# Scan layer and expert FFN on one core: new places for the first group's projections, for u x D, for the last sigmoid and for one FFN layer

## The chip, the cores and the metric

One core of one Trainium2 chip. The metric is the device time of one execution of the program in microseconds (us), the median of repeated runs.

## The reference, cut to what matters

32 sequences of 128 tokens, 128 features, all in fp32. Each goes through a rotation and a layer norm, a two-directional selective scan ("Mamba") with 256 channels and 16 states, a gated linear unit, a per-sequence low-rank expert layer, and an FFN of width 512:

```python
xc = conv(xi) + conv_b;  u = silu(xc)                     # forward, and reversed in time
dt, Bm, Cm = split(u @ x_proj_w.T)
delta = softplus(dt @ dt_proj_w.T + dt_proj_b)
h = exp(delta * A[n]) * h + (delta * u) * Bm[n]           # for each of 16 states n
y = sum over n of Cm[n] * h  +  u * D                     # u x D, the "skip"
y = y * silu(z);  o = gelu(both directions @ out_proj, dim_reduce)
g = o @ glu_w.T + glu_b;  x1 = g[:128] * sigmoid(g[128:]) + residuals
c = experts(x1)                                           # hid = relu(..), wo
f = silu(gate(c)) * up(c);  f = gelu(h1(f));  f = gelu(h2(f));  out = x1 + w3(f)
```

## The kernel before, in words

**Groups and units.** The sequences are taken in nine groups: group 0 and group 8 have 2 sequences (width 256), groups 1 to 7 have 4 (width 512). A group has 32 **units**: 16 states forward, then 16 in reverse; a unit handles both channel halves at once, so its tiles are 128 x 512 in the outer groups and 128 x 1024 in the inner ones. For a unit, POOL forms the drive du x B (L555), ScalarE the decay exp(delta x A) into one of two PSUM banks (L702), VectorE runs the scan along time (L905) and weighs it with C (L910); for 7 of the 32 units POOL does the weighing (L560) after a scan at L903. TensorE adds the units up by transposing each into `bank_y` (`sum_states`, L1190).

**Around the units.** After the 16th unit of a direction ScalarE copies `bank_y` out (`copy_y`, L708), TensorE turns it back and adds u x D with a matmul against a diagonal (`turn_y`, L1199 for the product, L1201 for the turn), and VectorE multiplies by silu(z) (`gate_y`, L921). All other TensorE work goes through two PSUM banks, `bank_m`: a **fill** is one product into the bank that is next in a fixed order, a **take** is ScalarE's (or VectorE's) read of it, and a fill waits until the fill two before it has been taken. Names of fills: norm, uf0, uf1, ur0, ur1 (convolution, forward and reverse, two halves), z0, z1, dbc, dt (steps and B, C), out, glu1, glu0, res, hid, wo, gate, up, h1, h2 (each of the last in four chunks), w3, tok. A group's front part (norm to dt) runs while the group before is scanned, its back part (out to tok) while the next is scanned. The last group's back part has nothing behind it: that is the **last chain**.

**The order of the work** is written out by a half-unit clock. Tables `FILL`, `TAKE_LAG`, `ACT_AT`, `VEC`, `GPS`, `LOADS`, `SETUP` give each step a time in units, and `FIRST_GROUP`, `NEXT_TO_LAST` and `LAST_GROUP` shift it for groups 0, 7 and 8 (`slot`, L131). Each engine walks the same clock (`timeline`, L354) and issues what has come due, so the tables fix only the order on each engine; semaphores do the rest. `SETUP` places the fills that merge the eight experts' low-rank factors (wi0 to wi7, wo0 to wo7) into full matrices, which VectorE takes (`merge`, L958), and `fuse`, one product of two weights.

**ScalarE's tables.** exp and ln are in one set of activation tables, silu in a second, gelu in a third; `use_table` (L584) loads a set where the next operation needs another (L586). From group 1 on, silu of both u's is one pass after the takes (`silu_front`, L651); in group 0 it is applied in each take (L644). In the last group gelu and silu are applied in the takes, elsewhere in one pass over four chunks (`gelu`, L754; `DIRECT`, L105). The sigmoid is exp at the take (L719), then ln and exp (L721 to L728).

**SP's queue** issues every DMA in the same clock: B and C are stored to memory by `store_bc` (L411) once dbc is taken, and read back as broadcast rows, and x, expert matrices and outputs go the same way.

**Group 0's way to the first scan.** rotation constants; VectorE's `conv_weights` (L878) and `skip_weights` (L873), then `rotate` (L880); POOL's power; ScalarE's `normalise`; norm; z1, z0, uf1, ur0, uf0, ur1 (the six fills in this order); dbc0, dt01, dt00; softplus (L685); POOL's `step_sizes` (delta, L535) and `inputs` (du, L544); then units.

## Time and profile before

| | |
|---|---|
| Median of 3 runs | 1063.78 us (1063.17 to 1065.88) |
| The profiled execution | 1062.9 us, span of its profile 1060.6 us |
| First scan of group 0 / 1 / 8 | 34.65 / 110.74 / 924.74 us |
| Last weighing ends, then the last chain | 1001.6 us, 59.0 us to the end |
| Busy share of the span | TensorE 89%, VectorE 86%, POOL 78%, ScalarE 73% |
| Granted TensorE clock, mean | 0.96 of full speed |

A row of the timeline reads: start, length, engine, line, operation, output<-input, shapes, number of instructions, and in brackets how long the engine had been idle and what released it. A matmul of fp32 stands as two instructions.

### The profile page before, as it was taken

To read this page: it belongs to the slowest core of one execution; us is meant where nothing else is said; L and a number is where in the kernel's file an instruction comes from. 1 tells how busy PE (TensorE), PEld (TensorE's weight loads), DVE (VectorE), ACT (ScalarE), POOL (GpSimd) and SP (SyncE) were. 2 spreads that over 40 slices of the span, in tenths; PEclk is the share of its full clock that TensorE was granted. 3 is DMA by queue.
4 is the path that set the end of the run, shared out by engine and by line. 5 is a ranking of instruction groups with operands and counts; after the bars stand their busy time and mean duration, and the time that the engine had idled before them with its cause. 6 is when DMAs were issued, how large, how long until landed. Compare 5 with 4: busy or idle time off the path is not lost.

```text
span 1060.6 us, 13662 instructions
## 1 busy us (share of the span) xinstructions
PE 943.8 (89%) x4312; PEld 599.0 (56%) x4312; DVE 908.4 (86%) x718; ACT 778.1 (73%) x1233; POOL 829.5 (78%) x430
## 2 busy tenths in 40 slices
PE   5698678778999899999999999999999988998987
PEld 3455455656655467445755566545755575556455
DVE  1788999999999989999999999998999999968600
ACT  4757667778698768877688868877788758777532
POOL 0767998989988897989878997979878998866300
PEclk9697699898999999999999999999999999999999
DMA  3766675463646555654556554745555465536000
GB/s 95 253 204 208 187 216 180 137 218 116 195 142 194 171 165 147 208 167 144 160 163 183 168 167 123 237 147 168 153 164 187 151 178 146 165 121 169 0 11 6
DMA packets 97670, 167.43 MB, mean 158 GB/s; under 512 B 9920, under 2 KB 33408, under 8 KB 97344
## 3 DMA queue, kind: packets, MB, share of 16 engines
q1 hardware_dynamic: 97600, 166.57, 50.8%
q8 instruction: 35, 0.57, 0.2%
q14 instruction: 35, 0.29, 0.1%
HBM read 159.19 MB, written 7.34 MB: 157 GB/s over the span
## 4 chain that ended last, share of the span: by engine, by line
PE 46%; DVE 19%; ACT 17%; issue 15%; POOL 3%; DMA 0%; DVEq 0%; SPq 0%; POOLq 0%; ACTq 0%
DVE bank_d L905 12%; PE bank_m L1102 9%; PE bank_m L1026 9%; PE bank_y L1190 8%; ACT L586 5%; ACT bank_d L702 5%; PE bank_m L1109 5%; PE bank_m L1116 2%; DVE state L903 2%; PE bank_m L1075 2%; PE bank_m L1084 2%; DVE state L910 2%; POOL state L555 2%; PE bank_m L1044 1%; PE bank_m L1059 1%
## 5 line engine op out<-in xcount | busy, mean ns | idle before, releaser
L555 POOL TENSOR_TENSOR state<-du,b_rows 128x1024 f32<-128x1024 f32 (+1 forms) x288 | 603.9, 2121 | 92.6 <-PE bank_y L1190 91.7
L905 DVE TENSOR_TENSOR_SCAN bank_d<-bank_d,state 128x1024 f32<-128x1024 f32 (+1 forms) x225 | 461.2, 2050 | 44.0 <-ACT bank_d L702 38.6
L702 ACT ACTIVATE bank_d<-delta,a_neg 128x512 f32<-128x512 f32 (+1 forms) x576 | 345.0, 634 | 104.5 <-DVE state L910 94.2
L1190 PEld LDWEIGHTS bank_y<-ident,state 128*128 128x128 f32 x2048 | 240.4, 145 | 81.7 <-issue 55.5
L1190 PE MATMUL bank_y<-ident,state 128*128 128x128 f32 x2048 | 263.3, 281 | 17.8 <-POOL state L560 11.7
L910 DVE TENSOR_TENSOR state<-bank_d,c_rows 128x1024 f32<-128x1024 f32 (+1 forms) x225 | 248.8, 1106 | 7.8
L560 POOL TENSOR_TENSOR state<-state,c_rows 128x1024 f32<-128x1024 f32 (+1 forms) x63 | 134.2, 2131 | 16.4 <-DVE state L903 16.4
L903 DVE TENSOR_TENSOR_SCAN state<-bank_d,state 128x1024 f32<-128x1024 f32 (+1 forms) x63 | 128.7, 2042 | 1.2 <-ACT bank_d L702 1.2
L1109 PE MATMUL bank_m<-hidA,h_s 128*128 128x512 f32 (+1 forms) x256 | 111.8, 584 | 15.6 <-ACT relu_dt L683 9.7
L1026 PE MATMUL bank_m<-xnT,w_conv 128*128 128x508 f32 (+7 forms) x288 | 115.3, 550 | 4.8 <-DVE x1T L930 3.1
L1102 PE MATMUL bank_m<-hidB,h_s 128*128 128x512 f32 (+1 forms) x256 | 110.3, 584 | 1.7 <-DVE hidB L944 0.8
L586 ACT ACT_TABLE_LOAD x69 | 88.5, 1283 | 1.9 <-PEq L1266 0.7
L1109 PEld LDWEIGHTS bank_m<-hidA,h_s 128*128 128x128 f32 x256 | 48.3, 197 | 69.3 <-issue 50.7
L1026 PEld LDWEIGHTS bank_m<-xnT,w_conv 128*128 128x128 f32 x288 | 54.1, 195 | 51.0 <-issue 43.1
L1102 PEld LDWEIGHTS bank_m<-hidB,h_s 128*128 128x128 f32 x256 | 48.5, 194 | 56.0 <-issue 52.3
L535 POOL TENSOR_TENSOR delta<-relu_dt,log_dt 128x1024 f32<-128x1024 f32 (+1 forms) x18 | 38.2, 2122 | 24.5 <-ACT log_dt L693 24.5
L1044 PE MATMUL bank_m<-dbc,w_dt_s 64*128 64x512 f32 (+1 forms) x72 | 37.5, 612 | 15.0 <-ACT dbc L677 12.6
L751 ACT ACTIVATE hidB<-bank_m,col 128x512 f32<-128x512 f32 (+1 forms) x32 | 21.1, 661 | 34.6 <-PE bank_m L1109 34.0
L921 DVE TENSOR_TENSOR gated<-bank_y,z 128x1024 f32<-128x1024 f32 (+1 forms) x18 | 19.8, 1102 | 26.5 <-PE bank_y L1201 26.5
L520 POOL TENSOR_TENSOR rstd<-var_eps,half_power 128x4 f32<-128x4 f32 (+1 forms) x9 | 8.6, 951 | 35.1 <-issue 20.1
L1075 PE MATMUL bank_m<-x1T,wsel 128*128 128x128 f32 x240 | 31.7, 278 | 3.9 <-DVE x1T L934 3.5
L1075 PEld LDWEIGHTS bank_m<-x1T,wsel 128*128 128x128 f32 x240 | 29.6, 191 | 7.7 <-DVE x1T L930 3.9
(143 smaller groups left out, 1011.8 us busy)
## 6 DMA issues: line engine op xcount, KB each, us to landing
b_rows<-bc_store SPq DMA_DIRECT2D x256, 256.0 KB, 4.2
c_rows<-bc_store SPq DMA_DIRECT2D x256, 256.0 KB, 4.3
wsel<-merged SPq DMA_DIRECT2D x32, 512.0 KB, 3.5
merged<-hidA SPq DMA_DIRECT2D x8, 512.0 KB, 3.1
h_s<-in_h SPq DMA_DIRECT2D x2, 1024.0 KB, 8.9
xin<-in_x SPq DMA_DIRECT2D x7, 256.0 KB, 3.9
out<-cT SPq DMA_DIRECT2D x7, 256.0 KB, 3.1
wsel<-in_factors SPq DMA_DIRECT2D x8, 160.0 KB, 3.7
```

The lines of the kernel that those rows point to most:

```text
L555: nc.gpsimd.tensor_tensor(split(unit_state(u)), du[:, d, :, :width(g)], per_half(b_rows, u), ALU.mult).then_inc(S.bx_ready, 1)
L560: nc.gpsimd.tensor_tensor(split(unit_state(u)), split(unit_state(u)), per_half(c_rows, u), ALU.mult).then_inc(S.weighed, 1)
L586: act.preload_act_table_set(name)
L702: ins = act.activation(split(unit_decay(u))[:, h], delta[:, d, h, :width(g)], ACT.Exp, scale=a_neg[:, h, n:n + 1])
L903: dve.tensor_tensor_scan(drive, decay, drive, 0.0, ALU.mult, ALU.add).then_inc(S.unit_done, 1)
L905: dve.tensor_tensor_scan(decay, decay, drive, 0.0, ALU.mult, ALU.add).then_inc(S.scanned, 1)
L910: dve.tensor_tensor(split(unit_state(u)), split(unit_decay(u)), per_half(c_rows, u), ALU.mult).then_inc(S.unit_done, 1)
L1026: ins = pe.matmul(dst, w, src, start=(m == 0), stop=(m == TAPS - 1))
L1075: ins = pe.matmul(bank(g, f"hid{f}")[:, at], wsel[:, s, f * P:(f + 1) * P], x1T[:, at], start=True, stop=True)
L1102: ins = pe.matmul(bank(g, f"h1_{f}"), h1_s[:, q, f * P:(f + 1) * P], hidB[:, q, :width(g)], start=(q == 0), stop=(q == FC - 1))
L1109: ins = pe.matmul(bank(g, f"h2_{f}"), h2_s[:, q, f * P:(f + 1) * P], hidA[:, q, :width(g)], start=(q == 0), stop=(q == FC - 1))
L1190: ins = pe.matmul(bank_y[:, h, s * P:(s + 1) * P], split(unit_state(u))[:, h, s * LEN:(s + 1) * LEN], ident[:, :], start=(n == 0 and s == ...
```

## The change

1. **Group 0.** The forward projections go first: norm, uf1, uf0, dbc0, dt00, dt01, and after them ur1, ur0, z0, z1 and the merges wi1 and wi0 (before: only wi1 ahead of the first scan); `fuse` follows the first scan. The reverse steps (dbc1, dt10, dt11, softplus and du of the reverse direction) move in among the units. The reverse u gets its silu in a pass with silu(z) after unit 5's decay, which needs a switch of tables there and back. VectorE forms delta and du of the forward direction (`first_inputs`) in POOL's place, and runs `rotate` of group 0 ahead of the two weight preparations.
2. **Groups 7 and 8.** ScalarE writes u x D into `gated` (`skip`: two copies with a scale of D), and TensorE adds it into `bank_y` by transposes ahead of the last state's; `turn_y` has no product against the diagonal any more.
3. **Last sigmoid.** 0.5 tanh(0.5 x) + 0.5, with tanh from gelu's table set: one take and one Identity.
4. **h2 of group 7.** Gelu in the takes, and the four fills are placed inside the last chain: h2_1 between turn and out, h2_0 between glu0 and res, h2_2 between hid and wo, h2_3 between wo and gate; w3 of group 7 follows gate2, and its tok the up fills. Before, all four stand ahead of the last turn.
5. The tables are given new values throughout, with a shift table for group 1; in the groups between, fills and takes change place by at most a few.

```diff
-SETUP = {"fuse": -8.0, "wi0": 4.0, "wo0": 3.5, "wi1": -5.5, "wo1": 5.0, "wi2": 10.0, "wo2": 10.5, "wi3": 12.0,
-         "wo3": 13.0, "wi4": 16.0, "wo4": 16.0, "wi5": 21.5, "wo5": 20.5, "wi6": 20.5, "wo6": 24.5, "wi7": 25.0,
-         "wo7": 25.5}
...
+SETUP = {"fuse": -2.0, "wi0": -7.0, "wo0": 4.5, "wi1": -7.5, "wo1": 3.5, "wi2": 10.5, "wo2": 12.5, "wi3": 10.5,
+         "wo3": 15.0, "wi4": 16.0, "wo4": 16.5, "wi5": 20.5, "wo5": 19.0, "wi6": 21.5, "wo6": 28.0, "wi7": 25.0,
+         "wo7": 24.5}
...
-ACT_AT = {"scale": -36.5, "normalise": -27.5, "softplus": (-6.0, 3.5), "copied": (18.5, 32.5), "silu": (-10.5, 52.0),
-          "sigmoid": 42.0, "gelu": (61.5, 71.0)}
+ACT_AT = {"scale": -36.5, "normalise": -27.5, "softplus": (-6.0, 4.0), "copied": (18.5, 32.5), "front": -10.5,
+          "silu": 52.0, "skip": (12.5, 26.0), "sigmoid": 42.0, "gelu": (61.5, 70.5)}
...
-LAST_GROUP = {"up0": 3.0, "uf1": 4.5, "h2_2": 3.5, "delta": -1, "ur0": -0.5, "h2_0": 9.5, "h2_1": 6.0, "h2_3": 4.0,
-              "w3": 3.0, "tok": 9.0, "gelu": -7, "up1": 8.5, "gate2": -0.5, "h1_2": 7.0, "up3": 8.0, "hid2": 0.0,
...
+FIRST_GROUP = {"ur1": 3.5, "h1_1": -3.0, "h2_0": 3.5, "power": 3.5, "bc_store": 0, "ur0": 8.0, "z0": 4.5, "z1": 7.0,
+               "dbc0": -11.0, "dt00": -9.5, "dt01": -10.0, "dbc1": 7.0, "dt10": 6.5, "dt11": 7.0, "out": 0.0, "glu1": 1.0,
+               "glu0": 0.0, "res": 0.5, "hid0": -2.0, "uf1": -3.0, "h1_0": 2.0, "h1_2": 1.0, "h2_2": -3.0, "up1": -0.5,
...
+LAST_GROUP = {"up0": 2.5, "uf1": 5.5, "h2_2": 10.5, "delta": -1, "ur0": 0.0, "h2_0": 19.0, "h2_1": 20.5, "h2_3": 10.0,
...
+NEXT_TO_LAST = {"res": 0.0, "residual": -2.5, "copied": 0.5, "h2_1": 4.5, "glu0": 0.0, "hid1": 1.5, "ur1": -1, "store": -4,
+                "sigmoid": 1, "h1_2": -1.5, "normalise": 0.5, "h1_0": 0.5, "h1_1": -2.0, "dbc1": 0.5, "x": 2, "selected": 1,
+                "z0": 2, "hid0": -2, "delta": 0.5, "h2_2": 13.5, "h2_3": 14.0, "norm": 0.0, "bc_store": -1.0, "w3": 10.0,
...
-DIRECT = {"gate": NG - 1, "h1_": NG - 1, "h2_": NG - 1}
+
+BY_SCALAR = NG - 2
+DIRECT = {"gate": NG - 1, "h1_": NG - 1, "h2_": NG - 2}
...
-                return act.activation(dst if d == 0 else dst[:, ::-1], bank(g, name), ACT.Silu if g == 0 else ACT.Identity, bias=c("conv_b", h))
+                return act.activation(dst if d == 0 else dst[:, ::-1], bank(g, name), ACT.Silu if g + d == 0 else ACT.Identity, bias=c("conv_b", h))
...
-                    if g > 0:
+                    if g + d > 0:
                         act.activation(u, u, ACT.Silu).then_inc(S.u_ready, 1)
...
+            def skip(g, d):
+
+                wait_u(act, g, d)
+                if g > 0:
+                    wait_filled(act, g - 1, "out")
+                w = width(g)
+                for h in range(HALVES):
+                    ins = act.activation(gated[:, d, h, :w], (u_f, u_r)[d][:, g % 2, h, :w], ACT.Copy, scale=c("skip_d", h))
+                ins.then_inc(S.skipped, 1)
+
...
+                if g == NG - 1:
+                    return act.activation(t, bank(g, "glu1"), ACT.Tanh, scale=0.5, bias=hb[:, 0:1])
...
+                if g == NG - 1:
+                    act.activation(t, t, ACT.Identity, scale=0.5, bias=half_col[:, 0:1]).then_inc(S.glu_ready, 1)
+                    return
...
+            def first_inputs():
+
+                w = width(0)
+                dve.wait_ge(S.log_ready, 1)
+                dve.tensor_tensor(delta[:, 0, :, :w], relu_dt[:, :, :w], log_dt[:, :, :w], ALU.add).then_inc(S.delta_ready, 1)
+                dve.wait_ge(S.delta_ready, 1)
+                wait_u(dve, 0, 0)
+                dve.tensor_tensor(du[:, 0, :, :w], delta[:, 0, :, :w], u_f[:, 0, :, :w], ALU.mult).then_inc(S.du_ready, 1)
 
...
+                if n == NST - 1 and g >= BY_SCALAR:
+                    pe.wait_ge(S.skipped, 2 * (g - BY_SCALAR) + d + 1)
+                    for h in range(HALVES):
+                        for s in range(sequences(g)):
+                            pe.matmul(bank_y[:, h, s * P:(s + 1) * P], gated[:, d, h, s * LEN:(s + 1) * LEN], ident[:, :],
+                                      start=False, stop=False, is_transpose=True, skip_group_check=True)
...
-                    pe.matmul(bank_y[:, h, :w], skip[:, h], (u_f, u_r)[d][:, g % 2, h, :w], start=True, stop=False, skip_group_check=True)
+                    if g < BY_SCALAR:
+                        pe.matmul(bank_y[:, h, :w], skip[:, h], (u_f, u_r)[d][:, g % 2, h, :w], start=True, stop=False, skip_group_check=True)
                     for s in range(sequences(g)):
                         ins = pe.matmul(bank_y[:, h, s * LEN:(s + 1) * LEN], y_rows[:, h, s * P:(s + 1) * P], ident[:, :],
-                                        start=False, stop=True, is_transpose=True, skip_group_check=True)
+                                        start=(g >= BY_SCALAR and s == 0), stop=True, is_transpose=True, skip_group_check=True)
```

## Rows read from the trace of the kernel before

**Rows 1.** Stretches of the run: length, busy time (instructions) of each engine, PEclk, DMA share, GB/s.

```profile
0.00:34.65 34.65, 18.21 (x64) 13.30 (x64) 6.01 (x26) 18.50 (x44) 6.16 (x14) 0.97 0.40 120
34.65:110.74 76.09, 66.50 (x260) 42.01 (x258) 66.55 (x85) 50.37 (x107) 58.16 (x47) 0.79 0.70 225
...
339.90:456.68 116.78, 109.60 (x510) 66.68 (x509) 110.47 (x77) 93.71 (x140) 102.64 (x48) 1.00 0.54 168
...
924.74:1001.60 76.86, 71.47 (x330) 43.44 (x328) 60.96 (x66) 54.34 (x100) 45.36 (x38) 1.00 0.37 106
1001.60:1016.90 15.30, 14.63 (x37) 6.77 (x38) 0.00 (x0) 3.73 (x5) 0.00 (x0) 1.00 0.00 0
1016.90:1060.60 43.70, 34.55 (x156) 25.23 (x155) 4.57 (x9) 16.76 (x28) 0.00 (x0) 1.00 0.03 10
```

**Rows 2.** Timeline, 0 to 36 us: start, length, engine, line, [idle before <-releaser].

```profile
6.30 1.23 DVE L878 TENSOR_TENSOR w_conv<-du 128x1024 f32<-128x1024 f32 x1 [0.69 <-DMA du<-in_w_in]
...
7.83 0.42 DVE L883 TENSOR_TENSOR xc<-xc,scaled 128x256 f32<-128x256 f32 x1
...
13.17 2.05 PE L1032 MATMUL bank_m<-xnT,w_z_s 128*128 128x256 f32 x4 [0.75 <-ACT xnT L634]
...
15.01 9.04 PE L1026 MATMUL bank_m<-xnT,w_conv 128*128 128x256 f32 x32
...
23.88 1.02 PE L1038 MATMUL bank_m<-u_f,w_x_s 128*96 128x256 f32 x4
...
29.72 0.72 ACT L693 ACTIVATE log_dt<-log_dt,one_col 128x512 f32<-128x512 f32 x1
...
31.86 1.27 POOL L544 TENSOR_TENSOR du<-delta,u_f 128x512 f32<-128x512 f32 x1
...
34.65 1.23 DVE L905 TENSOR_TENSOR_SCAN bank_d<-bank_d,state 128x512 f32<-128x512 f32 x1 [4.64 <-POOL state L555]
```

**Rows 3.** Matmuls of L1026 between 11 and 25 us: duration ns min/median/max.

```profile
L1026 PE MATMUL bank_m<-xnT,w_conv x32: 372/377/634, 15.0 to 23.7; 128*128 128x256 f32 x8, 128*128 128x254 f32 x8, 128*128 128x252 f32 x8, 128*128 128x250 f32 x8
```

**Rows 4.** Timeline of VectorE in the first group.

```profile
62.89 0.69 DVE L965 SCALAR_TENSOR_TENSOR hidA<-bank_m,hidB 128x512 f32<-128x512 f32 x1 [1.83 <-PE bank_m L1177]
...
83.73 0.69 DVE L921 TENSOR_TENSOR gated<-bank_y,z 128x512 f32<-128x512 f32 x1 [1.65 <-PE bank_y L1201]
...
94.81 1.23 DVE L905 TENSOR_TENSOR_SCAN bank_d<-bank_d,state 128x512 f32<-128x512 f32 x1 [1.89 <-ACT bank_d L702]
```

**Rows 5.** Timeline of TensorE in the first group.

```profile
54.34 7.03 PE L1026 MATMUL bank_m<-xnT,w_conv 128*128 128x512 f32 x16
```

**Rows 6.** Groups of instructions on the page: the table loads.

```profile
L586 ACT ACT_TABLE_LOAD x69 | 88.5, 1283 | 1.9 <-PEq L1266 0.7
```

**Rows 7.** Timeline of TensorE, 935 to 939 us.

```profile
935.56 1.02 PE L1199 MATMUL bank_y<-u_r,skip 128*128 128x512 f32 x2
936.42 0.60 PE L1201 MATMUL bank_y<-ident,ysum 128*128 128x128 f32 x4
```

**Rows 8.** Timeline of VectorE near the same turn and at the last chain.

```profile
938.36 1.23 DVE L921 TENSOR_TENSOR gated<-bank_y,z 128x1024 f32<-128x1024 f32 x1 [2.58 <-PE bank_y L1201]
...
1018.24 0.69 DVE L921 TENSOR_TENSOR gated<-bank_y,z 128x512 f32<-128x512 f32 x1 [16.69 <-PE bank_y L1201]
```

**Rows 9.** Timeline, 1001 us to the end.

```profile
1002.69 0.58 ACT L708 ACTIVATE ysum<-bank_y 128x512 f32<-128x512 f32 x1
...
1002.93 13.97 PE L1109 MATMUL bank_m<-hidA,h_s 128*128 128x512 f32 x32 [0.67 <-ACT hidA L758]
...
1021.53 1.28 ACT L586 ACT_TABLE_LOAD   x1
...
1022.16 3.60 PE L1116 MATMUL bank_m<-hidB,w_s 128*128 128x512 f32 x8
...
1027.72 2.52 PE L1075 MATMUL bank_m<-du,wsel 128*128 128x128 f32 x16
...
1039.38 7.14 PE L1102 MATMUL bank_m<-log_dt,h_s 128*128 128x256 f32 x32 [0.62 <-DVE log_dt L944]
```

More of the change, by code:

```diff
@@ L77 @@
 TURN = (19.0, 36.0)
-LOADS = {"x": -40.0, "bc_store": (-7.5, -0.5), "selected": (24.0, 26.5, 28.0, 30.0), "store": 78.0, "back": 3.5}
+LOADS = {"x": -40.0, "bc_store": (-7.5, 0.5), "selected": (23.5, 26.5, 28.5, 31.0), "store": 76.0, "back": 3.5}
 ROW_LEAD, C_LEAD = 6, 3
-FIRST_GROUP = {"ur1": -2.5, "h1_1": 1.0, "h2_0": 3.5, "power": 3.5, "bc_store": 1.0, "ur0": -0.5, "z0": -8.0, "z1": -8.0,
[5 rows of a table removed]
-               "gate1": -0.5, "delta": -0.5, "inputs": -1, "normalise": -1.0, "gated": -1.5, "back": 2, "sigmoid": -1.5}
@@ new lines @@
+LAST_GROUP = {"up0": 2.5, "uf1": 5.5, "h2_2": 10.5, "delta": -1, "ur0": 0.0, "h2_0": 19.0, "h2_1": 20.5, "h2_3": 10.0,
[4 rows of a table added]
+              "scale": -0.5, "glu1": -1.0, "store": 4.5, "norm": 0, "back": 3.5, "selected:2": 4, "gated:1": -2,
+              "selected": -2, "bc_store:0": -3.5, "skip:0": 4, "ur1": -0.5, "z1": 0.5, "dbc0": -1.0, "dt00": -1.0,
+              "copied:1": -0.5, "selected:3": -3, "sigmoid": -3.0, "gelu:0": 5.5, "delta:0": -0.5, "dt01": -1.0,
+              "bc_store:1": -2, "inputs:0": -0.5, "silu": -1}
@@ L280, in wait_u @@
         def wait_u(eng, g, d):
-            if g == 0:
-                wait_taken(eng, g, *(("uf0", "uf1"), ("ur0", "ur1"))[d])
+            if g + d == 0:
+                wait_taken(eng, g, "uf0", "uf1")
             else:
-                eng.wait_ge(S.u_ready, 2 * (g - 1) + d + 1)
+                eng.wait_ge(S.u_ready, 2 * g + d)
         def wait_hidden(eng, g, name):
@@ L827, in _ @@
                 for g, rel in groups[::-1]:
[L828 removed]
+                    if rel == slot(ACT_AT, g, "front"):
                         silu_front(g)
[L830 removed]
+                    if not direct(g, "gate") and rel == slot(ACT_AT, g, "silu"):
                         silu_gate(g)
                 for g, rel in groups[::-1]:
[L833 removed]
+                    if rel == slot(ACT_AT, g, "front"):
                         silu_z(g)
```

61 lines of the change are left out of this document (34 added, 27 removed), and 30 rows, old and new, of tables (FILL, FIRST_GROUP, LAST_GROUP, NEXT_TO_LAST).

## The prediction, made before the change was run

> **What bounds the kernel now.** I read the table of stretches first [rows 1]. An inner group lasts 116.78 us with VectorE busy 110.47 and TensorE 109.60: VectorE's scans set the pace, TensorE is close behind, and some 6 us of VectorE are idle. The first group is half as wide, and its 76.09 us hold only 66.55 of VectorE. Ahead of it stand 34.65 us with no scan, behind the last weighing 59.0 us (15.30 and 43.70) in which TensorE works 49.2. So the kernel is a head, nine scan stretches and a last chain; a gain in head or chain shows in full, one on a side engine in the middle doesn't. Next I read the timelines of the head [rows 2], of the first group's waits [rows 4, 5], of a turn near the end [rows 7, 8], and of the last chain [rows 9]; the order of each engine's work, old and new, I took from the tables of the diff.
>
> **The head.** (a) `rotate` waits at 7.83 behind the weight product that began at 6.30 [rows 2]. Put first, it gains between 0 and 1.53 us; I take 0.85, since ScalarE's last scaled tile comes only near 7. (b) z1 and z0 run from 13.17 to 15.01 ahead of the first convolution: 1.84 us go. uf1 starts near 12.3. (c) The 32 convolution matmuls take 8.87 us, 15.01 to 23.88 [rows 2], durations 372 to 634 ns [rows 3]. A 512-wide one goes by every 0.43 us at full speed (7.03 over 16, [rows 5]), a 256-wide one in 0.215, so 32 x 0.215 leaves 2.0 us: some nine ran at half speed, and the clock doubled near 19.0, although the granted clock of this stretch is shown as about full. Only 16 now stand before dbc0. If the doubling comes 0.85 earlier with the first product, they are done at 18.65; if it stays at 19.0, at 19.1; if it moves with uf1, at 17.75. With a take of 0.6, dbc0 starts at 19.25 (18.4 to 19.75) and not at 23.88: 4.6 us. (d) From dbc0 to the end of the log, 30.44, the steps are unchanged: 6.56 us, so 25.8. (e) POOL's two products of 1.27 us become two on VectorE, which needs 0.69 for a tile of that size [rows 4]: 1.3 us, and drive and decay could start the first scan near 28.7. (f) They don't set it. The new order puts two merges ahead of scan 0, and wi0's bank is that of z1. After the log ScalarE takes ur1, ur0, z0, z1 (about 2.0 us with the waits), then come wi0's fill, about 1.1, and its take, 0.69: scan 0 at 30.0 where it was 34.65. **Head: -4.65** (-4.0 to -5.5). B's way through memory starts with dbc0's take and is 4.6 us earlier as well; x of group 1 is now behind that store in SP's queue, lands near 25 and is wanted at 28.7, so it costs nothing.
>
> **The first group.** The merge that left the stretch is replaced by fuse's copy of equal length: no change. VectorE's idle time is 9.5 us now, of it 1.83 at a merge, 1.65 at the gate, 1.89 at a decay [rows 4]. New is ScalarE's block after unit 5's decay: two table loads of 1.28 [rows 6] and two silu of 0.62, 3.8 us. At that moment VectorE has rotate (2.5), scans 4 and 5 with weighing (1.86 each) and a merge ahead, 6.9 us in all, and the next decay is ready 5.5 us after unit 3: hidden; without rotate there it would cost 1 us. The Trainium skill, "ScalarE: Activation LUTs", "What ACT_TABLE_LOAD costs", puts a switch of tables at 2.66 us, load plus drain. By it the block would be 6.6 us and VectorE would stand some 1.4 us; the last chain would gain that again. The rows' 1283 ns, with the next operation right behind, are what I use. The reverse half of the front is now done here, on TensorE, which is light early on; its log comes after unit 11's decay, du of the reverse direction 4.8 us after unit 9, the drive 1.25 later, and VectorE wants it 6.2 after: just covered. The fills uf0 and ur0 of group 1 (6.9 us, [rows 5]) then start 3 us at half clock and hold decay 13 and the merges behind them, 1.2 us longer than today, but wi3 is then already merged and the 1.28 us of later merge waits and part of the gate's go. **First group: -1.3** (-4 to +3): the first scan of group 1 near 104.8.
>
> **Groups 1 to 6.** The few exchanges of fills and takes leave ScalarE's order round each wait of VectorE as it is; I count **-0.3** (-2 to +2) for all.
>
> **Groups 7 and 8.** A turn of 512 columns is two pairs of diagonal products and two fours of transposes, 2.6 us from 935.56 to 938.16 [rows 7]; without the products 0.9. Against that 8 transposes (0.87) come ahead of the last state. At the turn of 7.1 VectorE waits 2.58 [rows 8] and TensorE has been busy without a break, so the net 0.85 counts. At 8.0 the turn moves ahead of gate1 and gate2 and a wait of 1.7 goes, but the silu behind those gates binds, so 0.3. At 7.0 VectorE didn't wait: 0. The copies by ScalarE (0.67 each, 1.3 per direction; half in group 8) lie in its 22 idle us of a 76.86 us stretch; were they late, each would hold a decay by as much. **-1.2** (-3 to +2.5).
>
> **The last chain,** counted from the end of the copy of y, 1003.27 (1002.69 + 0.58, [rows 9]); today it ends 57.3 us later. Today: 13.97 us of h2, turn, gate at 1018.24 [rows 8], out, 1.28 us of table and ln/exp, w3 of group 7 (3.60), hid at 1027.72, h1 at 1039.38, and 21.2 from there to the end. New, in us from the copy: turn done 0.65, gated 1.4 beside h2_1, which runs 0.5 to 4.0 (13.97 over four, 3.44 each); out 4.0 to 5.9, gelu 6.4, glu1 7.2, tanh 7.75; h2_0 7.8 to 11.25, and beside it glu0's product; res and its sum 12.1; hid 12.2 to 14.5; h2_2 to 18.0; wo to 19.9; h2_3 to 23.25; w3 after its take 24.2 to 27.7; the remaining gates and ups through two banks, each waiting on the take two before, to 32.4; h1 at 32.5, end at 53.7. **Chain: -3.6.** The parts of that: 0.85 for the products of the turn, 0.8 the wait for the gate covered by h2_1, the rest the table load and the waits at res, hid and wo that h2 fills. From above: if all 8 us of TensorE's idle time in 1001.6 to 1060.6 but the serial end were filled, -6; from below, if each h2 fill just delays the step behind it and no wait is covered, only 0.85 and the table's 1.28 remain, with w3 now in series against it: -0.5.
>
> **Sum.** -4.65 -1.3 -0.3 -1.2 -3.6 = -11.05. The profiled execution took 1062.9 us (span 1060.6), 0.9 under the median of the runs; 1051.9 against it, and with the 0.9 back 1052.7. I forecast **1052.5**. Smaller than 0.3%, 3.2 us, a measurement of this kernel can hardly tell from no change.
>
> **Rivals.** *Head gain eaten by the first group* (chance 0.2): the reverse drive or the two convolution fills of group 1 come late and VectorE waits for them. For it: the cover of the reverse drive is under 0.2 us by my count, and the merge waits sit just there. Against: POOL is idle 18 of 76 us. Scan 0 at 30, group 1 still near 108 to 110: -6, 1058. *The last chain gains nothing* (0.1): fills of 3.44 us where the waits are 0.6 to 0.8. Then -0.5 in place of -3.6: 1056. *More than I count* (0.07): most of the first group's 9.5 idle us go as well, 1046. *Slower* (0.04): TensorE's clock. The first group's PEclk is 0.79 now [rows 1]; 66.5 x 0.79 = 52.5 us of work at full clock must fit its time. Reverse products trickle in among light transposes, just where the clock is low. The stretch may last 86.5 us (76.1 + 10.4) before all gains are gone, that is PEclk 52.5 / 86.5 = 0.61; at 0.55 it would be 95 us and the kernel 1072. Against: after unit 9 the convolutions come back to back as today. The Trainium skill, "TensorE: Matmul & The Clock Gate", "What you observe", says that the throttled clock is the default and activity lifts it, which would work against thinning TensorE's early work. *The change doing nothing* I leave out: its orders are fixed by the code.
>
> **Numbers.** The main case, 1049 to 1055.5, has 0.57; with the eaten head and the dead chain the range is 1047.5 to 1059.5. Faster 0.93, same 0.03, slower 0.04.
>
> **What would show it.** Right: first scan near 30.0, with the take of wi0 just ahead of it; dbc0 near 19.3; first scan of group 1 near 105; inner groups at 116.8 to 118.5; no L1199 product after group 6; 70 table loads (two more, one less); end 53 to 54 us after the last copy of y, TensorE nearly unbroken there. Wrong: a first scan at 32 or later (clock or bank), a VectorE wait over 3 us between scans 12 and 18, PEclk under 0.7 in the first group, a last chain over 56 us, or a changed period of the inner groups, which I hold fixed.

## The result, and the profile after

The changed kernel took **1068.53 us** (median of 20 runs, 1064.7 to 1074.39) against 1064.14 (20 runs, 1062.82 to 1066.09) for the kernel before: ratio **1.0045** [1.0032, 1.0058], so 0.45% slower. The forecast was 1052.5, faster. The profiled execution of the changed kernel took 1068.88 us; its span was 1066.7 where that of before was 1060.6.

The table of stretches, cut at the first scan of each group, at the last weighing's end and at the end of the run (length; busy time and instructions of TensorE, its weight loads, VectorE, ScalarE, POOL; PEclk; DMA share; GB/s):

```profile
0.00:30.64 30.64, 16.27 (x57) 11.08 (x58) 7.38 (x29) 16.42 (x39) 5.05 (x12) 1.00 0.47 140
30.64:113.15 82.51, 69.40 (x268) 41.95 (x266) 66.55 (x85) 55.23 (x115) 57.95 (x47) 0.77 0.65 205
113.15:225.97 112.82, 84.98 (x412) 60.46 (x413) 107.71 (x78) 82.59 (x132) 105.03 (x49) 0.86 0.61 188
225.97:345.52 119.55, 111.26 (x518) 71.95 (x518) 110.53 (x78) 91.68 (x140) 103.67 (x49) 0.94 0.55 167
345.52:464.24 118.72, 111.42 (x509) 67.56 (x508) 110.68 (x77) 93.65 (x140) 102.50 (x48) 0.99 0.53 165
464.24:581.57 117.33, 111.17 (x509) 67.62 (x508) 110.70 (x78) 93.66 (x140) 102.52 (x48) 0.99 0.54 167
581.57:700.89 119.32, 112.01 (x510) 67.76 (x509) 110.76 (x77) 93.53 (x140) 103.16 (x48) 0.99 0.53 164
...
818.76:934.07 115.31, 102.77 (x513) 68.72 (x512) 109.68 (x73) 88.12 (x133) 98.63 (x49) 0.97 0.56 158
934.07:1010.20 76.13, 70.01 (x334) 43.58 (x332) 60.74 (x66) 55.82 (x104) 46.47 (x39) 1.00 0.36 112
1010.20:1066.70 56.50, 48.26 (x192) 31.40 (x192) 4.77 (x10) 17.20 (x30) 0.00 (x0) 0.99 0.03 8
```

Against before [rows 1]: the head is shorter by 4.01, the first group longer by 6.42, with VectorE busy for the same 66.55. The inner groups have VectorE at 110.5 to 110.8 as before, but last up to 119.5. The last stretch (59.0 before) is shorter by 2.5. From first scan to first scan, group by group, in us (the first scan of each group in VectorE's timeline; the last column runs to the end of the last group's last scan):

| kernel | first scan | 0 | 1 | 2 | 3 | 4 | 5 | 6 | 7 | 8 |
|---|---|---|---|---|---|---|---|---|---|---|
| before | 34.65 | 76.1 | 112.6 | 116.5 | 116.8 | 118.5 | 117.1 | 118.5 | 114.0 | 76.1 |
| after | 30.64 | 82.5 | 112.8 | 119.5 | 118.7 | 117.3 | 119.3 | 117.9 | 115.3 | 75.5 |

The head (start, length, engine, line of the changed kernel, idle and releaser):

```profile
13.24 5.91 PE L1076 MATMUL bank_m<-xnT,w_conv 128*128 128x256 f32 x16 [0.65 <-ACT xnT L652]
19.76 1.07 PE L1088 MATMUL bank_m<-u_f,w_x_s 128*96 128x256 f32 x4 [0.61 <-issue]
...
30.04 0.69 DVE L1012 SCALAR_TENSOR_TENSOR hidA<-bank_m,hidB 128x512 f32<-128x512 f32 x1 [0.24 <-PE bank_m L1227]
30.64 1.22 DVE L952 TENSOR_TENSOR_SCAN bank_d<-bank_d,state 128x512 f32<-128x512 f32 x1
```

Sixteen convolution matmuls stand ahead of dbc0, which begins at 19.76 (23.88 before, [rows 2]); the take of wi0 is the last thing ahead of the first scan. The loss follows, in TensorE's timeline of the first group (four of its rows):

```profile
80.62 2.07 PE L1230 MATMUL bank_m<-wsel 32*128 32x128 f32 x8
82.62 2.08 PE L1082 MATMUL bank_m<-xnT,w_z_s 128*128 128x512 f32 x2
...
87.05 3.67 PE L1246 MATMUL bank_y<-ident,state 128*128 128x128 f32 x16
...
93.56 3.24 PE L1088 MATMUL bank_m<-u_f,w_x_s 128*96 128x512 f32 x4
```

and in the windows around it:

```profile
75.00:80.00 5.00, 4.31 (x19) 3.23 (x18) 4.04 (x6) 2.33 (x5) 3.62 (x3) 0.58 0.91 262
80.00:85.00 5.00, 4.69 (x13) 2.51 (x11) 4.23 (x5) 0.28 (x2) 0.00 (x0) 0.50 0.66 223
85.00:90.00 5.00, 4.95 (x16) 3.45 (x17) 3.81 (x5) 4.97 (x8) 1.69 (x2) 0.50 0.09 38
90.00:95.00 5.00, 5.00 (x12) 2.29 (x11) 2.75 (x4) 3.30 (x5) 5.00 (x5) 0.50 0.87 249
```

From about 76 us, just ahead of the turn, to 96, TensorE is busy nearly all the time and granted 0.50, the lower of its two levels (1.2 GHz). Each row takes about twice its time at full clock: 16 transposes 3.67 us, where in before they took 1.97. VectorE's waits there are 1.13, 2.22 and 2.91 us. The last convolution product ahead of this stretch ended at 70.6 us, in before at 76.7, with the clock at 1.00 in both.

In the inner groups much of the new time stands at single waits. In group 3 it is one wait for a decay (VectorE), behind h1 matmuls that took 5.40 us for eight (TensorE, second fence):

```profile
444.18 2.29 DVE L950 TENSOR_TENSOR_SCAN state<-bank_d,state 128x1024 f32<-128x1024 f32 x1 [1.60 <-ACT bank_d L720]
```

```profile
436.83 5.40 PE L1152 MATMUL bank_m<-hidB,h_s 128*128 128x512 f32 x8
```

ScalarE had waited 4.06 us for that product, with the decay queued behind its take. Group 4, with the same orders, had no such wait and took 117.3. The kernel before has two such rows as well, in its groups 4 and 6, the two that take 118.5 us in its trace:

```profile
547.85 5.40 PE L1102 MATMUL bank_m<-hidB,h_s 128*128 128x512 f32 x8
```

The last chain (timeline of ScalarE and TensorE, answering [rows 9]):

```profile
1012.15 0.66 PE L1258 MATMUL bank_y<-ident,ysum 128*128 128x128 f32 x4 [0.69 <-ACT ysum L736]
1012.64 3.60 PE L1159 MATMUL bank_m<-hidA,h_s 128*128 128x512 f32 x8
...
1018.62 1.10 PE L1109 MATMUL bank_m<-xnT,w_glu_s 128*128 128x256 f32 x4 [0.66 <-ACT xnT L740]
1019.86 3.70 PE L1159 MATMUL bank_m<-hidA,h_s 128*128 128x512 f32 x8
...
1045.44 7.14 PE L1152 MATMUL bank_m<-log_dt,h_s 128*128 128x256 f32 x32
```

```profile
1019.33 0.47 ACT L749 ACTIVATE du<-bank_m,hb 128x256 f32<-128x256 f32 x1 [0.85 <-PE bank_m L1109]
1019.84 0.51 ACT L757 ACTIVATE du<-du,half_col 128x256 f32<-128x256 f32 x1
```

The turn has no product left, h2 of group 7 stands in four pieces between the chain's steps, tanh needs no table load. The copy of y ended at 1012.10: 54.6 us to the end, where before had 57.3.

### The profile page after: what moved, and what is told of

Its sections match the earlier page's. It is cut to its first block, busy times and chain, and to the rows that moved or that the text cites. A ratio compares the mean times of both kernels' runs of the same rounds, so it can differ in the third digit from the quotient of the medians.

```text
span 1066.7 us, 13706 instructions
## 1 busy us (share of the span) xinstructions
PE 946.9 (89%) x4320; PEld 598.9 (56%) x4320; DVE 910.2 (85%) x722; ACT 780.5 (73%) x1241; POOL 826.9 (78%) x428
## 4 chain that ended last, share of the span: by engine, by line
PE 49%; ACT 18%; DVE 17%; issue 12%; POOL 4%; DMA 0%; DVEq 0%; ACTq 0%; POOLq 0%
DVE bank_d L952 11%; PE bank_y L1246 10%; PE bank_m L1152 8%; PE bank_m L1076 8%; PE bank_m L1159 6%; ACT L604 5%; ACT bank_d L720 5%; POOL state L573 3%; PE bank_m L1166 2%; PE bank_m L1125 2%; DVE state L957 2%; PE bank_m L1094 2%; DVE state L950 2%; PE bank_m L1088 2%; PE bank_m L1134 2%
## 5 line engine op out<-in xcount | busy, mean ns | idle before, releaser
L1159 PE MATMUL bank_m<-hidA,h_s 128*128 128x512 f32 (+1 forms) x256 | 114.4, 594 | 17.5 <-ACT relu_dt L701 10.6
L1152 PE MATMUL bank_m<-hidB,h_s 128*128 128x512 f32 (+1 forms) x256 | 111.5, 589 | 1.6 <-ACT relu_dt L701 0.9
L780 ACT ACTIVATE hidA<-bank_m,col 128x512 f32<-128x512 f32 (+1 forms) x32 | 20.7, 651 | 29.6 <-PE bank_m L1152 29.6
```

The lines of the kernel that those rows point to most:

```text
L1152: ins = pe.matmul(bank(g, f"h1_{f}"), h1_s[:, q, f * P:(f + 1) * P], hidB[:, q, :width(g)], start=(q == 0), stop=(q == FC - 1))
L1159: ins = pe.matmul(bank(g, f"h2_{f}"), h2_s[:, q, f * P:(f + 1) * P], hidA[:, q, :width(g)], start=(q == 0), stop=(q == FC - 1))
```

## The experiments

All were timed beside the kernel before; a ratio is to that. The group lengths come from one profiled execution of each kernel. "New" and "old" orders mean the tables of slots of the changed kernel and of the kernel before. Kernels that mix them take each group's slots from one set:

```diff
 def slot(table, g, name, k=None):
...
+    if g not in NEW_GROUPS:
+        table = OLD_OF[id(table)]
+        at = table[name] if k is None else table[name][k]
...
```

The projections of a group stand up to 25 units ahead of its first scan, so a group's tables act partly in the group ahead of it. Where group 0 is old, the code of the head is as before too.

**e1 to e4: the parts.** NEW_GROUPS (0, 1) with the new setup; (2, ..., 6); (7, 8) with u x D by ScalarE, tanh and h2 in the chain; (0, 1, 7, 8).

> Groups 0 and 1 and the merges with the new orders (forward projections first, delta and du on VectorE, silu of the reverse u in a pass), everything from group 2 on as before. Theory A (the first group gives the head back through TensorE's clock): first scan near 30.6, first scan of group 2 about 2.6 us later than before, total 1066 to 1067. Theory B (the orders of groups 2 to 6 cost the time, the head is a gain): first scan of group 2 not later than before, total 1060 or less.

> Only groups 2 to 6 with the new orders, both ends as before. Theory A: the inner groups are as long as before within 1 us in all, total 1063 to 1065. Theory B: they are 5 us longer in all as in the changed kernel, total 1068 to 1070.

> Only groups 7 and 8 with the new orders, with u x D by ScalarE, the tanh and h2 of group 7 inside the last chain. If the last chain gains the 2.7 us seen in the changed kernel and groups 7 and 8 cost the 0.8 seen there: 1062. If all of the 3.6 and 1.2 that were forecast come: 1059. If the ScalarE copies cost more than the products: 1064 or more.

> The whole change with the old orders for groups 2 to 6 alone. Theory A (first group): only 0 to 1 us better than the changed kernel, 1067 to 1069. Theory B (inner orders): 5 us better than the changed kernel, 1063.

| | ratio | first scan | 0 | 1 | 2 | 3 | 4 | 5 | 6 | 7 | 8 |
|---|---|---|---|---|---|---|---|---|---|---|---|
| e1 | 1.0026 [1.0014, 1.0039] | 30.5 | 82.4 | 112.8 | 118.3 | 120.3 | 117.1 | 118.5 | 117.7 | 114.0 | 77.5 |
| e2 | 1.0025 [1.0016, 1.0035] | 33.7 | 77.7 | 110.9 | 118.5 | 117.3 | 118.7 | 118.7 | 117.3 | 114.0 | 77.3 |
| e3 | 1.0047 [1.0028, 1.0066] | 34.0 | 77.8 | 113.3 | 116.7 | 116.8 | 118.5 | 117.8 | 121.0 | 117.1 | 77.3 |
| e4 | 1.0069 [1.0045, 1.0093] | 30.0 | 82.3 | 111.5 | 116.4 | 117.1 | 118.5 | 117.8 | 121.0 | 117.1 | 77.3 |

No part alone is a gain. Whenever the head is new, the first group takes over 82. e2 prices the new inner orders by themselves: 0.25%, 2.7 us. The profiled execution of e1 was the slowest of its twelve (1071.07, median 1068.2); its groups 2 to 6 have the old orders and took 591.8 us in sum, where in e5 the same orders took 587.4, so a single trace is no price for them.

In e3 and e4 groups 6 and 7 lose 5.6 together, which the trace of the whole change doesn't have (117.9 and 115.3). I put that to the seam between an old group 6 and a new group 7. For group 6 this isn't shown: its eight h1 matmuls took 5.40 us in both, and e12 below, which has no seam, shows the same row and 121.1 us. Whether the seam has a part in group 7's 117.1 is open. So e3 and e4 say little about the tail.

**e5: control.** NEW_GROUPS empty.

> Control. Every group has the orders of the kernel before on all engines, written in the changed kernel's source (the two constants for tanh are still made in the setup). Theory (the mixed kernels cost what their orders cost, and the writing nothing): ratio to the kernel before 1.000, within 0.001; first scan within 1 us of 34.65; group lengths of 76 to 78, 111 to 113, then as before within 1 us each. Rival (the writing itself, or chance from one profile to the next, moves the inner groups by microseconds): ratio above 1.0015 or a group length off by 2 us, and then the +2.0 to +3 us seen for one group in a mixed kernel prove nothing.

Ratio 1.0001 [0.9986, 1.0015]: the writing costs nothing. Its profile has 77.8 and 113.9 for groups 0 and 1 (before: 76.1 and 112.6), so these two move by over a microsecond from one execution to another. Groups 2 to 8 repeat within 0.2 in these two; e12 below has groups that move by up to 3.2.

**e6: two projections put back.**

```diff
+OVER = {(1, 'ur1'): -17.5, (1, 'z0'): -18.5}
...
+    if key in OVER:
+        return OVER[key]
```

OVER sets single slots. In the changed kernel ur1 of group 1 stands at -19.0 and z0 at -13.0.

> The changed kernel, with two projections of group 1 put back where they were, ahead of the turn of the first group: the second half of the reverse convolution at -17.5 and the first half of z at -18.5 of its group (-19.0 and -13.0 in the changed kernel). The work of TensorE is the same in sum. Theory (TensorE's clock): in the changed kernel the granted clock was 0.50 from about 77 to 97 us, where before it was back at 1.00 by 85, and the same matmuls took twice as long (8 transposes' pair of rows 3.67 us for x16 against 1.97); with streaming projections next to the turn as before, the clock comes back by 87, and the first group takes 78 to 79.5 us in place of 82.5: time 1064.5 to 1066.5. Rival (work moved from the head into the first group: TensorE simply has 3 us more to do there, in whatever order): first group 82 to 83, time unchanged at 1068.5.

Median 1065.32, 3.2 under the changed kernel's; ratio 1.0014 [0.9997, 1.0032]. First group 78.1 in place of 82.5, group 1 110.8 in place of 112.8; the profiled execution was the fastest of twelve (1062.31), so these two differences are larger than that of the medians. TensorE's timeline, then the windows:

```profile
79.93 1.15 PE L1278 MATMUL bank_m<-wsel 32*128 32x128 f32 x8
...
81.87 1.97 PE L1294 MATMUL bank_y<-ident,state 128*128 128x128 f32 x16
...
87.09 1.93 PE L1136 MATMUL bank_m<-u_f,w_x_s 128*96 128x512 f32 x4 [0.93 <-DVE hidA L1060]
```

```profile
80.00:85.00 5.00, 4.34 (x28) 3.13 (x28) 4.94 (x7) 2.98 (x7) 2.33 (x2) 1.00 0.89 288
85.00:90.00 5.00, 3.54 (x14) 1.49 (x12) 4.15 (x6) 4.97 (x5) 3.88 (x4) 1.00 0.47 154
90.00:95.00 5.00, 3.27 (x8) 1.38 (x8) 3.82 (x5) 4.37 (x10) 2.61 (x3) 0.79 0.75 230
```

The same merge takes 1.15 and not 2.07 us, the transposes 1.97 and not 3.67, the dbc product starts 6.5 us earlier. The same work in another order keeps the upper level (2.4 GHz) until 93 us, where the changed kernel lost it at 76: the theory of the clock holds, the rival (more work, whatever its order) falls. It repeats. With the new head and the two slots as changed, the first group took 82.3 to 82.5 in all four traces (the changed kernel, e1, e4, e8); with the two put back, 77.6 to 79.2 in all nine (e6, e9 to e12, e14, e15, e17, e18). Why TensorE loses the clock behind the one order and not behind the other isn't shown.

**e7: the same by added work.** On the changed kernel; ur1 of group 1 stays at -19.0.

```diff
+OVER = {(1, 'z0'): -13.5}
...
             def fill_z(g, h):
...
+                for _ in range(4 if (g, h) == (1, 0) else 0):
+                    pe.matmul(bank(g, f"z{h}"), w_z_s[:, h * P:(h + 1) * P], xnT[:, :width(g)], start=True, stop=True)
```

The edit does two things: it adds four matmuls, and it moves z0 by half a unit, from behind the turn to ahead of it.

> The changed kernel, with the first half of z of group 1 moved ahead of the turn of the first group, and issued five times over in place of once (the results of the first four are overwritten): four matmul pairs more, 4 x 1.1 = 4.4 us of added TensorE work at full clock. Theory (clock): more streaming work just ahead of the turn keeps the granted clock up through 80 to 97 us, where some 10 us of matmuls now take 16 to 17; the gain of 6 pays for the added 4.4, so that the first group comes out at 80.5 to 83 although it does more. Rival (TensorE's amount of work sets the group): first group 86 to 87, time 1072 to 1073.

```profile
76.81 4.78 PE L1131 MATMUL bank_m<-xnT,w_z_s 128*128 128x512 f32 x8
81.43 1.02 PE L1132 MATMUL bank_m<-xnT,w_z_s 128*128 128x512 f32 x2
...
85.63 1.97 PE L1296 MATMUL bank_y<-ident,state 128*128 128x128 f32 x16
...
90.85 1.93 PE L1138 MATMUL bank_m<-u_f,w_x_s 128*96 128x512 f32 x4 [1.03 <-DVE hidA L1060]
```

With 4.78 us of useless matmuls ahead of the turn, the 16 transposes start 1.4 us and the dbc product 2.7 us earlier than in the changed kernel, and the first group lasts 82.2, not longer than 82.5. The expectation for the group holds. The ratio, 1.0053 [1.0036, 1.0070], is no gain: what the clock gives back the added work takes. How much of it the added work gave back and how much the move of z0 alone, this run can't tell.

**e8: u x D by TensorE in the new orders.**

```diff
-BY_SCALAR = NG - 2
+BY_SCALAR = NG
```

> The changed kernel with its orders, but the product u x D of groups 7 and 8 made by TensorE again at the turn, as before; tanh and h2 in the last chain stay. Theory (ScalarE is what the end of the scans waits for in groups 7 and 8, and the four copies of u x D, 2 x 1.2 us for group 7 and 2 x 0.65 for group 8, cost it more than the 2.3 us that TensorE's products take at a turn): groups 7 and 8 together shorter by 1 to 3 us (115.3 + 75.5 now), time 1066 to 1067.5. Rival (the turn is the tight place, as forecast: product at the turn on the way to the weighing by z): longer by 1 to 2 us, time 1069.5 to 1070.5.

Ratio 1.0056 [1.0034, 1.0079], not to be told from the changed kernel's 1.0045; groups 7 and 8 at 117.2 and 77.0 (115.3 and 75.5). The theory, a gain without the copies, finds no support. But the 3.4 us between the two traces aren't the price of the copies: e7, e9, e11 and e12 have these orders with ScalarE's copies and took 116.9 and 77.0. What goes with the longer group 7 is its eight h1 matmuls: 3.70 us where the group takes 115.3, 4.46 in e8 and 4.37 to 4.56 in those four. So the copies are worth between 0.3 and 3.4 us within these orders. Two things of e8 do repeat: the gate of turn 7.1 comes 13.7 us after the first scan of group 8 and not 12.8, and the chain from the copy is 55.5 and not 54.6. Two terms of the forecast, 0.85 each, are met.

**e9: groups 2 to 5 old, on e6.** NEW_GROUPS (0, 1, 6, 7, 8).

> The kernel of e6 (changed kernel, two projections of group 1 put back), with groups 2 to 5 in the orders of the kernel before on every engine. Theory (the new orders of the inner groups cost time by themselves: 469.0 us for groups 2 to 5 in the control, 474.7 in e6): groups 2 to 5 take 468.5 to 471, time 1060 to 1062, ratio to the kernel before 0.996 to 0.998. Rival (the inner groups lose because they stand behind a changed head, whatever their own orders): groups 2 to 5 stay at 473 or more, or the two seams give it back, time 1064 to 1066.

Median 1063.09, ratio 0.9986 [0.9970, 1.0002]; groups 2 to 5 at 118.1, 117.0, 118.5, 117.9, 471.5 in sum. Between the two: 3.2 us less than e6, though 2.5 above the control's 469.0. The time stays above the 1060 to 1062 of the theory and under the rival's 1064.

**e10: the idle ahead of h1 filled, on e6.**

```diff
             def fill_dt(g, d, h):
+                if d + h == 0 and 2 <= g < NG - 1:
+                    pe.matmul(bank(g, "dt00"), w1_s[:, 0:P], h1_s[:, 0, 0:width(g)], start=True, stop=True)
                 wait_taken(pe, g, f"dbc{d}")
```

> The kernel of e6, with one matmul added ahead of the first delta projection of each of groups 2 to 7, while TensorE waits there for ScalarE's copy of dbc (1.39 us of idle): weights by weights, 128x128 by 128x512, into the bank that is just opened, overwritten by the projection. Its 1.0 us lie in that idle. Theory (clock): in groups 3 and 5 of e6 the h1 matmuls right behind this idle fell to the lower clock (x8 in 5.40 us against 3.70 where it did not) and scan 26 then waited 1.60; with the idle filled that does not occur: groups 3 and 5 take 117.3 in place of 118.7 and 119.3, time lower by 3 although TensorE does 6 us more: 1061.5 to 1063.5. Rival (scan 26 waits for something in the order, the clock is by-play): groups 3 and 5 unchanged at 118.7 or longer, time 1065 to 1068.

```profile
427.14 1.02 PE L1142 MATMUL bank_m<-h_s,w_s 128*128 128x512 f32 x2
428.60 1.12 PE L1144 MATMUL bank_m<-dbc,w_dt_s 64*128 64x512 f32 x2 [0.44 <-ACT dbc L743]
429.65 3.70 PE L1202 MATMUL bank_m<-hidB,h_s 128*128 128x512 f32 x8
```

Median 1062.48 with all 12 runs in 1061.22 to 1063.59 (e6: 1062.31 to 1070.79); ratio 0.9977 [0.9966, 0.9989]. The eight h1 matmuls take 3.70, scan 26 no longer waits, groups 3 and 5 take 117.0 and 117.6 in place of 118.7 and 119.3. More work, less time: group 3's wait was the clock's, since all five traces with the changed kernel's orders in the inner groups, its head, and no filler in them (the changed kernel, e6, e7, e8, e12) have 5.40 there and take 118.7. Group 5 is less sure: without a filler it took 117.9 in e7 and e12. Groups 4 and 6 came out 1.2 and 1.7 longer than e6's; groups 2 to 6 together gained 2.4.

**e11: a filler meant for the wait ahead of group 2.** Four more such matmuls ahead of the first h2 projection of group 1.

> The kernel of e6, with four matmuls (4.1 us) added ahead of the first h2 projection of group 1, where TensorE is idle for 5.86 us before it waits for gelu's result. Theory (clock): after that idle the eight h2 matmuls took 3.75 us and the dbc ones 2.90, against 1.9 and 1.9 at full clock, and the second scan of group 2 waited 2.53; with the idle filled it waits under 0.8: group 2 takes 117.3 to 118 in place of 119.4, time lower by 1.5 to 2: 1063 to 1064. Rival (the order sets that wait): group 2 unchanged at 119.4, time 1065.3.

It missed its place: the idle at 218 us belongs to h2 of group 0. The matmuls ran at 338 us, where TensorE had no idle time; group 3 took 122.1 in place of 118.7, the kernel 1.0025 [1.0013, 1.0037]. What it shows: in a full stretch 3.6 us of TensorE (the eight rows from 338.51) cost 3.4.

**e12: the sigmoid without tanh, on e6.**

```diff
-HEAD, SETUP_NEW, TANH = True, True, True
+HEAD, SETUP_NEW, TANH = True, True, False
...
-                if g == NG - 1:
+                if TANH and g == NG - 1:
                     return act.activation(t, bank(g, "glu1"), ACT.Tanh, scale=0.5, bias=hb[:, 0:1])
                 return act.activation(t, bank(g, "glu1"), ACT.Exp, scale=-1.0, bias=hb[:, 1:2])
```

> The kernel of e6, with the last sigmoid by exp, ln and exp as before (two more passes and a table load at the end of the last chain). Forecast for tanh by the rows of before: it saves a table load of 1.28 us and one pass of 0.4 us in the last chain. Theory: last chain longer by 1.5 to 2.2 us, time 1067 to 1067.5. Rival (another product of the chain ends last there, so that the sigmoid is beside it): last chain longer by under 0.5 us, time unchanged at 1065.3.

```profile
1017.80 1.28 ACT L652 ACT_TABLE_LOAD   x1
...
1020.57 1.28 ACT L652 ACT_TABLE_LOAD   x1
1023.36 0.69 ACT L833 ACTIVATE hidB<-bank_m,col 128x512 f32<-128x512 f32 x1 [1.50 <-PE bank_m L1207]
```

The copy of y ended at 1011.40, the run at 1066.5: a chain of 55.1, only 0.5 longer (median 1066.39, ratio 1.0015 [0.9998, 1.0032]): the rival's reading. The first load lies in the 0.85 us that ScalarE waits for glu1 and sticks out of it by 0.4; the second lies beside an h2 fill.

e12 is also a second look at e6: up to the last sigmoid the two have the same orders. Their groups 2 to 8 took

| kernel | 2 | 3 | 4 | 5 | 6 | 7 | 8 |
|---|---|---|---|---|---|---|---|
| e6 | 119.4 | 118.7 | 117.3 | 119.3 | 117.9 | 115.3 | 75.5 |
| e12 | 117.6 | 118.7 | 118.7 | 117.9 | 121.1 | 116.9 | 77.0 |

So a group can differ by 3.2 us between two traces with no difference in its orders. For groups 2, 4, 5, 6 and 7 the row that differs is a TensorE product at the one or the other clock. In e12 (TensorE; group 2's reverse dbc, then h1 in groups 6 and 7):

```profile
221.90 1.88 PE L1136 MATMUL bank_m<-u_r,w_x_s 128*96 128x512 f32 x4
```

```profile
787.59 5.40 PE L1200 MATMUL bank_m<-hidB,h_s 128*128 128x512 f32 x8
```

```profile
905.96 4.55 PE L1200 MATMUL bank_m<-hidB,h_s 128*128 128x512 f32 x8
```

**e13, e14: both fillers,** on the control and on e9, the second one this time eight small matmuls ahead of the h2_1 projection of group 0.

> Not a variant of the change: the orders of the kernel before in every group (the control), with two fillers of matmuls whose results are overwritten: one of 1.0 us ahead of the first delta projection of groups 2 to 7, and eight of 0.5 us ahead of the first h2 projection of group 0, where TensorE was idle for 4.2 us just before group 2. Theory (the old orders are hardly hit by the clock in groups 2 to 6, so that the filler mends nothing there): no faster than the control, ratio 0.999 to 1.002. Rival (the filler is a gain of its own, and what e10 gained over the kernel before is not the change's): ratio 0.998 or less.

> The kernel of e9 (changed kernel, two projections of group 1 put back, groups 2 to 5 in the old orders), with the two fillers of e13. In the kernel of e11 the filler stood ahead of the first h2 of group 1, in the middle of group 3, where TensorE was not idle (that group: 122.1 in place of 118.7); the idle of 5.9 us before group 2 belongs to the h2 of group 0. Theory (clock): the wait of 2.5 us at the second scan of group 2 goes (group 2 at 116 to 117.5 against 118.1), the rest as e9's; time 1060 to 1062, ratio 0.996 to 0.998, and a spread of runs under 3 us where e9's is 8.5. Rival (fillers delay more than they save): 1063 or more.

The second filler missed again: group 0 begins its h2 with h2_2, and the added 3.6 us stood behind it. In e14 (TensorE, VectorE):

```profile
227.16 3.62 PE L1208 MATMUL bank_m<-h_s,w_s 128*128 128x256 f32 x16
```

```profile
237.19 2.29 DVE L998 TENSOR_TENSOR_SCAN state<-bank_d,state 128x1024 f32<-128x1024 f32 x1 [3.18 <-ACT bank_d L768]
```

Group 2 took 121.4 in e13 and 120.9 in e14 (control 116.7, e9 118.1). Ratios 1.0046 [1.0031, 1.0061] and 0.9987 [0.9975, 0.9999]. With the first filler alone at work, groups 3 to 6 of e13 were 2.0 shorter in sum than the control's: it may help the old orders as well, and then e10's lead over the kernel before isn't the change's alone.

**e15: the head alone, mended.** e1 with e6's two slots.

> The kernel of e1 (head and groups 0 and 1 in the new orders, all else old; ratio 1.0026) with the two projections of group 1 put back as in e6. Theory (what the new head gains is lost in the first group to the clock, by where those two stand): first group 78 to 79.5 in place of 82.4, group 1 at 111, the rest as the control: time 1060.5 to 1062.5, ratio 0.996 to 0.998. Rival (another loss takes its place): ratio 1.000 or more.

Median 1061.61 (9 runs), ratio **0.9973** [0.9963, 0.9984]; first scan 30.12, first group 79.2, group 1 111.5, groups 2 to 8 within 0.4 of the control's each. As the theory had it.

**e16: the tail alone, with its seam at group 6.** NEW_GROUPS (6, 7, 8).

> The end of the change alone, with its seam one group earlier than in e3: groups 6, 7 and 8 in the new orders with u x D by ScalarE, tanh and h2 in the last chain; groups 0 to 5 and the setup old. Theory (in e3 the old orders of group 6 beside the new ones of group 7 made the loss: 121.0 and 117.1 us against 118.5 and 114.0): group 6 at 118, group 7 at 115.3, group 8 at 75.5, last chain 54.6 from the end of the copy of y against 57.3 before: time 1062.5 to 1064, ratio 0.998 to 1.000. Rival (the tail in the new orders costs as much as it gains, wherever the seam is): group 7 at 117, time 1066 or more.

Ratio 1.0040 [1.0027, 1.0052]. The profiled run was the fastest of five (1065.13): groups 6, 7 and 8 at 118.0, 115.2 and 75.5 and a chain of 54.6 as the theory said, but group 5, into which group 6's projections reach, at 119.6 (control 117.0), with its eight h1 matmuls at 5.40 us. The other four took 1068.0 to 1069.3 at a mean granted clock of 0.947 and 0.948 in place of 0.953; no trace shows where. Against the theory's time, undecided in its parts.

**e17, e18: the chain's part alone, then ScalarE's copies, on e15.**

```diff
 def slot(table, g, name, k=None):
...
-    if g not in NEW_GROUPS:
+    if g not in NEW_GROUPS and not at_the_end(table, g, name, k):
         table = OLD_OF[id(table)]
```

at_the_end holds for h2, its gelu, w3, tok and the store of group 7 and for what group 8 does from its output projection on.

> The kernel of e15 (new head, groups 0 and 1 new with the two projections put back; ratio 0.9973) with only the chain's part of the change added: tanh, and h2, w3 and tok of group 7 inside the last chain, group 8's orders from its output projection on the new ones. The scans of groups 7 and 8 keep the old orders, and TensorE makes u x D. Theory (the last chain gains 2.7 us from the end of the copy of y by itself: 54.6 against 57.3, as in e6): last chain 54.5 to 55.2, scans as in e15, time 1058.5 to 1060, ratio 0.994 to 0.996. Rival (the old orders had h2 of group 7 where the scans waited anyway, and in the chain it delays what the scans of group 8 leave behind): last chain 56.5 or more, time 1061.5 or more.

> The kernel of e17 with u x D of groups 7 and 8 by ScalarE (at 12.5 and 26.0 of the group), the scans' orders old. Forecast of this step: 1.5 us gained at the three turns that scans stand behind, 1.2 us of ScalarE for each copy pair of group 7 lost where scans wait for it. Theory (in the old orders ScalarE is what the scans of groups 7 and 8 wait for): groups 7 and 8 longer by 1 to 4 us (114.0 and 76.1 in e15; e3 had 117.1 and 77.3), time 1060 to 1063. Rival (as e8 showed in the new orders, ScalarE's copies gain 3.4 us over TensorE's products): shorter by 1 us or more.

e17: median **1058.74** (1058.53 to 1060.73), ratio **0.9942** [0.9921, 0.9963], faster than both kernels and inside the theory's times. The chain lasts 55.5 from the copy's end, 0.3 over the expected range: TensorE's product is still in the turn, as in e8. e18: 1060.34 (1058.64 to 1060.89), ratio 0.9946 [0.9925, 0.9967], by the times not to be told from e17; groups 7 and 8 at 115.1 and 76.7 (114.0 and 76.1), the chain 54.6. By the traces the copies cost 1.7 on the old orders and return 0.9.

## Why the prediction was wrong

From trace to trace the forecast was -11.05, the measurement +6.1. Term by term:

**Head, forecast -4.65, measured -4.0: right but for 0.6.** The step that was off is (a): rotate came 0.67 earlier, but the first transposes did not, behind POOL's power, which took 1.54 us (0.71 before). The convolution starts at 13.24, where z stood before; that is (b) alone. (c) held: 5.91 us for 16 matmuls, 2.47 over the 3.44 of full speed, puts the doubling at 18.2. (d) took 6.60 against 6.56. (f) held: wi0's take at 30.04 is what the scan at 30.64 follows; it was forecast for 30.0.

**First group, forecast -1.3, measured +6.4: the step that failed.** I let group 1's two convolution fills "start 3 us at half clock" and costed z nowhere. The cost came later, at the turn, and from the clock. The cause is where two projections of group 1 stand: in e6 the same work in another order takes 4.4 us less in this group and 2.0 less in the next (3.2 less between the medians), e15 is e1 with those two slots alone changed and goes from 1.0026 to 0.9973, and in e7 added work is done sooner. The rival *slower* named this mechanism, at 0.04, but placed it among the early products and made its deciding point an average, PEclk 0.61 over the stretch. The average was 0.77, and some 20 us at 0.50 where merges, sums and dbc are queued back to back were enough. Its 10.4 us of gains outside this group are also a slip: the terms add up to 9.75. *Head gain eaten* foresaw the outcome with another cause: the reverse drive, which was in time.

**Groups 1 to 6, forecast -0.3, measured +5.7: failed.** "The exchanges leave ScalarE's order round each wait as it is" is true and beside the point: the term had nothing for TensorE's clock, and nothing for the orders by themselves, which e2 prices at 2.7 us. Of the 5.7, group 1 has 0.2, group 2 has 3.0, groups 3 to 6 have 2.5.

In group 2 the clock and the orders can be told apart. Its reverse dbc product took 3.08 us in the changed kernel and 1.88 in before. With the new orders and 1.88 (e10, e12) the group takes 117.5 and 117.6, with the old orders and 1.88 116.3 to 116.7 in seven traces (before, e3, e4, e5, e15, e16, e17). So some 1.9 us are the clock's and 1.1 the orders'; with the old orders and a slow product (e1, e9, e18) it takes 117.6 to 118.3. What brings the slow product about is open: behind the 5.79 us of idle ahead of it the h2 matmuls of group 0 took 3.75 us for eight where 1.89 is full speed, but the old orders have slow h2 there too (3.47 behind 4.35 us of idle), and both fillers missed the place.

In groups 3 to 6 both kernels have two groups with h1 at 5.40 us, 3 and 5 now, 4 and 6 before. The falls of the clock say which groups are long, not why the sum is 2.5 more. What each exchange does there, and how much is chance between executions (the same four groups with the old orders took 473.5 us in e1, as much as the changed kernel's 473.2; 470.8 in before), is open.

**Groups 7 and 8, forecast -1.2, measured +0.5.** The turn's 0.85 was met (e8: 0.9). Not met was "in its 22 idle us", which I had read from group 8's stretch alone: in group 7 decays do wait for ScalarE, and the stretch is 1.3 longer. e18 prices the copies on the old orders at +1.7, e8 only between -0.3 and -3.4 in the new ones; my term had one price for both. The +0.5 was itself a lucky trace: e7, e9, e11 and e12, with the same orders, took 3.1 more in these two groups.

**Last chain, forecast -3.6, measured -2.5** (from the copy's end -2.7). The turn's products gave 0.9 (e8), tanh 0.5 (e12) and not the table's 1.28 with more, the rest, some 1.3, is h2's filling of waits. The mis-sized term is tanh: without it one load lies in the wait for glu1 but for 0.4 us, the other beside TensorE's h2, which the new order had put there. These chain lengths repeat: 57.3 to 57.4 in six traces with the old chain, 54.5 to 54.6 in eleven with the new one.

Together 0.6 + 7.7 + 6.0 + 1.7 + 1.1 us of error make the 17.1 between -11.05 and +6.1. Four fifths stand in the first and the inner groups. The traces lay 4.4 in the first group and 1.9 in group 2 to TensorE's clock; the rest is the orders', chance between executions, or open.
